# First attention of a fused kernel: maxima taken earlier, their turn moved to another PSUM bank, and the value product spread over two units

## The reference

```python
def _mha(q, k, v):                       # q: layer-normed x; k = v: the context, 1024 rows a batch
    qh, kh, vh = ...                     # 16 heads of 32 columns
    scores = einsum('bhqd,bhkd->bhqk', qh, kh) / sqrt(32)
    causal = ki <= qi + (Sk - Sq)        # Sq = 512, Sk = 1024
    scores = where(causal, scores, -10000)
    attn = softmax(scores)
    return einsum('bhqk,bhkd->bhqd', attn, vh)
x = x + _mha(_layernorm(x), ctx, ctx)
x = x + _L0_ffn(_layernorm(x))           # 8 experts, top 2
x = x + _L1_xattn(_layernorm(x), ctx)    # 8-bit rounded q, k, v and weights of attention
x = x + _L1_ffn(_layernorm(x))           # rounded, gated
```

## Time and profile before

| | us |
|---|---|
| median of 3 runs | 1800.56 |
| lowest and highest | 1793.37 and 1804.84 |
| the profiled execution | 1805.99 |
| its span, from the first to the last instruction | 1804.4 |
| mean granted TensorE clock, as a share of full speed | 0.827 |

### The profile page before, as it was taken

One profiled execution on the slowest core, in us unless ns is written; L12 is line 12 of the kernel. 1 busy time (PEld: TensorE's weight loads), 2 busy tenths in 40 slices (PEclk: granted clock), 3 DMA queues, 4 the chain that ended last, 5 costly groups with the idle time before them and its releaser, 6 DMA issues.

```text
span 1804.4 us, 23942 instructions
## 1 busy us (share of the span) xinstructions
PE 1441.1 (80%) x8264; PEld 708.2 (39%) x8312; DVE 1037.8 (58%) x1668; ACT 771.5 (43%) x1017; POOL 420.4 (23%) x318
## 2 busy tenths in 40 slices
PE   6888057777777439999999999928788888887878
PEld 3444034444444314444444444414223333334334
DVE  5777868787788511111111111156799999993895
ACT  3544357777777201111111111103677777772453
POOL 1100000000000055799994000031111111110241
PEclk9988579999999669999999999969555555557989
DMA  5556443333332099999999888843899999996001
GB/s 178 156 161 192 157 93 81 78 76 76 76 79 51 1 341 400 368 386 376 404 407 336 302 303 302 244 143 75 163 206 211 215 216 213 213 205 138 1 1 47
DMA packets 469011, 345.96 MB, mean 192 GB/s; under 512 B 382040, under 2 KB 384088, under 8 KB 468320
## 3 DMA queue, kind: packets, MB, share of 16 engines
q1 hardware_dynamic: 454160, 295.76, 59.7%
q0 software_dynamic: 10816, 40.90, 7.2%
q10 hardware_dynamic: 3984, 8.65, 1.3%
HBM read 206.32 MB, written 38.27 MB: 136 GB/s over the span
## 4 chain that ended last, share of the span: by engine, by line
PE 43%; DVE 25%; issue 13%; DMA 9%; ACT 5%; POOL 3%; SPq 1%; DVEq 1%; POOLq 0%; ACTq 0%
PE scores L891 18%; PE bank L907 9%; DVE arena L1612 6%; DVE arena L1426 6%; DMA arena<-arena 6%; DVE arena L1440 3%; DMA arena<-in_ctx 2%; PE scores L747 2%; PE bank L815 2%; ACT arena L1226 2%; PE bank L899 1%; PE bank L1078 1%; PE bank L799 1%; PE bank L936 1%; PE bank L798 1%
## 5 line engine op out<-in xcount | busy, mean ns | idle before, releaser
L1612 DVE TENSOR_SCALAR_CACHE_REDUCE arena<-scores,arena 128x1024 f32<-128x1024 f32 x256 | 318.4, 1282 | 33.5 <-ACT arena L1226 15.2
L891 PE MATMUL scores<-arena 128*128 128x512 f32 x736 | 321.7, 595 | 0.8 <-DVE arena L1549 0.8
L952 PE MATMUL scores<-arena 96*128 96x512 bf16 x512 | 263.7, 621 | 50.8 <-DVE arena L1612 38.0
L1226 ACT ACTIVATE arena<-arena 128x2048 int16<-128x2048 f32 x128 | 256.2, 2002 | 101.2 <-POOL arena L684 76.3
L1557 DVE TENSOR_TENSOR arena<-scores,arena 128x512 f32<-128x512 f32 x46 | 31.8, 692 | 447.2 <-PE scores L891 447.2
L891 PEld LDWEIGHTS scores<-arena 128*128 128x128 f32 x736 | 140.6, 191 | 178.0 <-issue 176.8
L907 PE MATMUL bank<-arena 128*128 128x512 f32 x368 | 163.3, 597 | 3.5 <-issue 3.3
L1165 ACT ACTIVATE arena<-bank 128x512 f32<-128x512 f32 (+3 forms) x256 | 118.5, 512 | 50.8 <-PE bank L799 40.4
L1426 DVE TENSOR_REDUCE arena<-scores 128x1 f32<-128x640 f32 (+3 forms) x128 | 127.6, 1019 | 14.1 <-PE scores L776 13.9
L1194 ACT ACTIVATE arena<-scores 128x512 f32<-128x512 f32 x46 | 27.5, 597 | 248.9 <-PE scores L891 248.9
L1440 DVE TENSOR_TENSOR arena<-arena 128x1024 f16<-128x1024 f32 (+2 forms) x128 | 127.7, 1018 | 1.6 <-ACT arena L1170 1.6
(11 more groups left out here) (231 smaller groups left out, 2023.6 us busy)
## 6 DMA issues: line engine op xcount, KB each, us to landing
arena<-in_L_ffn_w SPq DMA_DIRECT2D x69, 2048.0 KB, 12.4
arena<-arena SPq DMA_DIRECT2D x32, 256.0 KB, 3.2
kst_d<-arena POOLq DMA_DIRECT2D x16, 384.0 KB, 5.4
tern_d<-arena POOLq DMA_DIRECT2D x12, 512.0 KB, 7.1
arena<-kst_d SPq DMA_DIRECT2D x16, 384.0 KB, 4.3
xs_d<-arena SPq DMA_DIRECT2D x23, 256.0 KB, 3.5
arena<-xs_d SPq DMA_DIRECT2D x23, 256.0 KB, 13.4
ys_d<-arena ACTq DMA_DIRECT2D x23, 256.0 KB, 7.0
```

The lines of the kernel that those rows point to most:

```text
L891: ins = pe.matmul(scores[:, m * 1024 + half * 512:m * 1024 + half * 512 + 512], xsT[a][:, c], wa[:, m, c, half * 512:half * 512 + 512], st ...
L952: ins = pe.matmul(scores[:, s:s + 512], qhead[a][0:K3, t * P:(t + 1) * P], khead[a][0:K3, s:s + 512], start=True, stop=True)
L1226: act.activation(p16[t % PBUF], ssb[i], ACT.Exp, bias=ebias[i], scale=-1.0, accum_out=rsum[a][:, t:t + 1]).then_inc(p_ready, 1)
L1612: dve.tensor_scalar(ssb[i][:, s:s + 1024], scores[:, s:s + 1024], nsq[:, bass.ds(h, 1), t], None, ALU.mult, ALU.min, accum_out=nmx[i][:, h ...
```

## The change

- **DVE.** In step u the remainders of groups 1 to 3 now belong to unit u-1 and stand first; then come the maxima 0 and 1 of unit u+1, `finish_unit(u-1)`, maximum 2, the remainder of group 0 of unit u, maximum 3 and `split_m(u+1)`. So all four maxima of u+1 are taken ahead of three of the four subtractions of u. `take_max(u, 0)` has a new wait for `m_step`, a semaphore that DVE itself raised.
- **PE.** `turn_m(u)` opens step u; `smax(u+1, 1)` follows, then `pv` of groups 1 to 3 of unit u-1, wrapped around the first scores of unit u; `pv` of group 0 of unit u closes the step, and behind it stands `smax(u+2, 0)`.
- **Bank.** `turn_m` writes to `bank6`, `copy_m` reads it there. The wait of `smax` for `m_ready` goes; one wait for `ctxT_ready` ahead of all units is added, since `bank6` served the context before.
- **ACT.** `copy_m(u+1)` stands ahead of the last `p1` copy of unit u, behind it before.

No instruction is added to the data path and none is taken away. SP's and GpSimd's queues are as before.

```diff
@@ tensor @@
-                    if past(u, 1):
-                        pe.wait_ge(m_ready, at(u - 1))
...
-                view = scores[:, 0:512].bitcast(BF16)
+                view = bank6[:].bitcast(BF16)
...
             def att_unit(u, a, r, first, last):
                 b, rb = (a + 1) % 4, r + (a + 1) // 4
+                c, rc = (a + 2) % 4, r + (a + 2) // 4
+                d, rd = (a + 3) % 4, r + (a + 3) // 4 - 1
+                turn_m(u, a)
                 if not last:
-                    smax(u + 1, b, 0, rb); smax(u + 1, b, 1, rb)
+                    smax(u + 1, b, 1, rb)
+                if not first:
+                    pv(u - 1, d, 2, rd, not past(u, 2)); pv(u - 1, d, 3, rd, not past(u, 2))
+                st(u, a, 0, first, r); st(u, a, 1, first, r)
+                if not first:
+                    for k in range(4, KT):
+                        pv(u - 1, d, k, rd, not past(u, 2))
                 st(u, a, 2, first, r); st(u, a, 3, first, r)
                 if not last:
                     smax(u + 1, b, 2, rb)
                 st(u, a, 4, first, r); st(u, a, 5, first, r)
-                pv(u, a, 0, r, first); pv(u, a, 1, r, first)
                 if not last:
                     smax(u + 1, b, 3, rb)
                 st(u, a, 6, first, r); st(u, a, 7, first, r)
-                pv(u, a, 2, r, first); pv(u, a, 3, r, first)
-                if not last:
-                    turn_m(u + 1, b)
-                    st(u + 1, b, 0, False, rb); st(u + 1, b, 1, False, rb)
-                pv(u, a, 4, r, first); pv(u, a, 5, r, first)
-                pv(u, a, 6, r, first); pv(u, a, 7, r, first)
+                pv(u, a, 0, r, first); pv(u, a, 1, r, first)
+                if within(u + 2, UNITS):
+                    smax(u + 2, c, 0, rc)
+                if last:
+                    for k in range(2, KT):
+                        pv(u, a, k, r, first)
@@ scalar @@
+                    if g == 3 and not last:
+                        copy_m(u + 1, b)
                     act.wait_ge(exp_done, KT * u + 2 * g + 2)
...
-                if not last:
-                    copy_m(u + 1, b)
@@ vector @@
+                if t == 0 and past(u, 1):
+                    dve.wait_ge(m_step, 2 * u)
...
                 if not first:
-                    finish_unit(u - 1, not past(u, 2))
+                    for g in range(1, 4):
+                        rest_of_p(u - 1, g)
                 if not last:
                     take_max(u + 1, 0)
                     take_max(u + 1, 1)
-                rest_of_p(u, 0)
+                if not first:
+                    finish_unit(u - 1, not past(u, 2))
                 if not last:
                     take_max(u + 1, 2)
-                rest_of_p(u, 1)
+                rest_of_p(u, 0)
                 if not last:
                     take_max(u + 1, 3)
                     split_m(u + 1, False)
-                rest_of_p(u, 2)
-                rest_of_p(u, 3)
```

More of the change, by code:

```diff
@@ L842, in _ @@
                 smax(0, 0, t, 0)
-            turn_m(0, 0)
-            st(0, 0, 0, True, 0); st(0, 0, 1, True, 0)
+            smax(1, 1, 0, 0)
+            pe.wait_ge(ctxT_ready, at(NC - 1))
             sweep4(pe, UNITS, att_unit)
@@ L1155, in copy_m @@
                 act.wait_ge(m_turned, at(u))
-                act.activation(qC[b][K2:K2 + 2].rearrange("p t n -> p (t n)"), scores[:, 0:512].bitcast(BF16)[K2:K2 + 2, 0:SQ], ACT.Copy).then_inc(m_ready, 1)
+                act.activation(qC[b][K2:K2 + 2].rearrange("p t n -> p (t n)"), bank6[:].bitcast(BF16)[K2:K2 + 2, 0:SQ], ACT.Copy).then_inc(m_ready, 1)
             def att_unit(u, a, k, first, last):
@@ L1465, in att_unit @@
                     split_m(u + 1, False)
-                rest_of_p(u, 2)
-                rest_of_p(u, 3)
                 if last:
+                    for g in range(1, 4):
+                        rest_of_p(u, g)
                     finish_unit(u, False)
```

## The result

| | before | changed |
|---|---|---|
| median of 4 runs each, us | 1802.7 | 1738.68 |
| lowest and highest | 1793.37 and 1807.64 | 1736.86 and 1740.34 |
| the profiled execution | 1805.99 | 1737.13 |
| its span | 1804.4 | 1735.5 |

The ratio is 0.9671 with a 95% interval of 0.9641 to 0.97: faster by 3.3%, and inside the range forecast (1738 to 1769), but by only 0.7 us.

A forecast was written before the change was run, and what follows sets the result against it. A wait for `pv`, no full engine, was taken to bound the first attention. Steps -53.9, clock +3, first step -1, last stretch +0.5 sum to -51.4; beside the median 1800.56 that gives 1749, rounded to 1750, range 1738 to 1769.

The forecast's parts named there:

- What bounds the stage: First attention: no engine is full; a wait sets the 10.85 us unit, VectorE idling 1.68 until TensorE's `pv` is done.
- The sum of VectorE's step, 8.91: VectorE, first attention: same instructions in another order, costs taken start to start, 8.91 us a step.
- Full durations in a row: VectorE: if the new neighbours were held, 0.09 more at some six places, 0.5 a unit and 15 us in all.
- The walk: One step followed from its first remainder: `finish_unit` free by 0.26, maximum 2 without margin, the turn free by 0.1.
- The 0.14 a step: Small waits at maximum 2 and the turn, added to 8.91 for a step of 9.05 us.
- The clock in the stage: TensorE, first attention: two falls of the clock expected at 1.5 each, +3 us, with 0 and +8 as ends.
- The ends: First step -1 us (0 to -2); behind the last split +0.5, for one more `pv` tail.
- all later stages keep their length: Stages behind the first attention: no change in time expected.
- A: Scores late at maximum 2, which has no margin: 0.5 more in each step, 15 us, 1764; 17%.
- B: TensorE's clock falls in nearly every unit of the first attention, 1.6 each: 1794; 7%.
- D: Slower: TensorE stays at 1.2 GHz through the first attention, 107 us more, 1907; 4%.
- C: Another wait takes the whole place: the turn 1.7 us later than walked, 48 us, 1797; 4%.

The follow-up runs named there:

- The experiment with 0.44 us more: Changed kernel with two unread matmuls of 512 columns into bank 6 ahead of `smax(u+1, 2)`, 0.44 us a unit: 30 steps 283.15 us, median 1755.98, ratio to before 0.977.

## Why the prediction was right, step by step

- **What bounds the stage** was read rightly: the loop of split, turn, copy, scores, `pv` and finish, with 1.68 us in which VectorE had nothing to put beside it. `finish_unit` set ahead of the maxima brings 1.2 us of idle time back in each unit, and 38.8 of the 55.2 us.
- **The sum of VectorE's step, 8.91,** from start-to-start distances of the earlier trace rows: three of four steps in the loop are 8.90 to 8.94. The new neighbours start as early as the old ones did. Three remainders in a row take 2.69, which is 1.22 + 1.09 + 0.55 less twice 0.09, to a hundredth. Full durations in a row would have made the step 9.4, by the estimate in the prediction. That is what the Trainium skill's rule on emptying the pipe (VectorE: DVE Perf Modes, The DRAIN you can't avoid) gives for held operations; the trace shows the other case of that section, in which the next one starts earlier. Outside the loop and in the kernel with the loop written out the same 8.91 is in part luck. The 0.15 inside `finish_unit` isn't there, so VectorE alone would need some 0.15 less; but maximum 2 starts 0.36 behind the multiply and not 0.24 as in the loop, since its scores are not there sooner. The loop over TensorE and ScalarE, which is 8.91 too, was not in the prediction at all; it compared TensorE's work alone, 7.2, with VectorE's. In the last steps of the changed kernel, outside the loop:

```profile
493.46 0.17 DVE L1456 RECIPROCAL arena<-bank 128x4 f32<-128x4 f32 x1
493.66 0.29 DVE L1458 TENSOR_TENSOR arena<-arena 128x128 f32<-128x128 f32 x1
494.02 1.09 DVE L1434 TENSOR_REDUCE arena<-scores 128x1 f32<-128x896 f32 x1
```

- **The walk.** Maximum 2 was to start at 5.23 to 5.25 and started at 5.24. The place without margin was the right one. The 0.14 a step added for it and the turn was not needed: 30 x 0.14 = 4.2 us too many. The turn was walked wrongly: at 0.15 and free by 0.1, but it started at 0.49, since `smax(u+2, 0)` ahead of it ended late. With it `copy_m` came at 0.92 and not at 0.57, and the last `p1` copy ended at 2.05, not 1.7, so the third remainder had 0.09 to spare and not 0.4. This cost nothing in the changed kernel, where `pv` of group 1 came at 1.28, as walked (1.27).
- **The loop.** Left out of the forecast: the jump back costs VectorE 0.47 every fourth step, and the loop 2.9 us in all. In the old order, where the wait for `pv` follows the jump, every fourth step is longer by only 0.03 (10.68 and 10.65). Together with the 4.2 us too many, 271.5 was forecast for 30 steps and 270.2 measured, by two errors that cancel for the most part.
- **The clock in the stage.** Two falls at 1.5 were expected, none came in the 30 steps: 3 us less than forecast, at the lower end of that term.
- **The ends.** -1 was forecast for the first step and -2.1 measured; +0.5 for the last stretch and +1.7 measured. The clock is in both. The first step took 8.86 us at a mean clock of 0.78 in one profile of the changed kernel and 7.87 at 1.00 in the other; before it was 10.97 at 0.66 and 10.64 at 0.71. The last stretch, from the split of unit 31 to the last `finish_unit`, took 10.74 or 10.75 in all four profiles of the old order. With the new order it took 11.48 or 11.49 in all six profiles in which the clock stayed at 1.00 there, so the change costs 0.7 in it, near the 0.5 forecast. The other 0.9 is a fall of the clock behind the last split, at 514 to 518 us, which shows in the last wait for `pv`: 1.55 here, 0.62 where the clock stayed up. `finish_unit` of the last unit but one waits 1.23 for `pv`, in either case. From the changed kernel's timeline, and then one us of it, beside the same us of the kernel with `smax` 0 not ahead:

```profile
506.60 2.69 DVE L1448 TENSOR_TENSOR arena<-arena 128x1024 f16<-128x1024 f32 x3
510.52 0.56 DVE L1454 TENSOR_REDUCE arena<-bank 128x128 f32<-128x384 f32 x1 [1.23 <-PE bank L813]
...
518.72 0.56 DVE L1454 TENSOR_REDUCE arena<-bank 128x128 f32<-128x384 f32 x1 [1.55 <-PE bank L813]
```

```profile
515.00:516.00 1.00, 1.00 (x16) 1.00 (x14) 0.44 (x1) 0.97 (x3) 0.00 (x0) 0.50 0.00 0
```

```profile
515.00:516.00 1.00, 1.00 (x27) 1.00 (x25) 0.32 (x2) 1.00 (x3) 0.00 (x0) 1.00 0.00 0
```

- **The rest of the miss.** On the profiled execution -51.4 was forecast. The stage and its ends gave -55.7, the later stages +1.0, and the context stage -14.2. The last was no term of the prediction: "all later stages keep their length" was said, and held within 1 us, but of the stage ahead I took for granted that it stands still. Its clock moves it by 14 us in the kernel before, and by 9 in the one profile with the new order that has a lower clock there. Against the medians the time came out 11 us below 1750. 4 of it are the stage with its ends, as the profiles show. The other 7 are not shown stage by stage: the forecast stands beside a median of three runs of before, 1800.56, of a kernel whose runs reach from 1789.5 to 1810.9 with the mean clock, and four runs of the changed kernel lay close together, three of them at a mean clock of 0.834 or more. By the profiles at equal clock the change is worth 55 us, not 64.
- **The rivals.** A (scores late): its place was right, and it cost nothing. The experiment with 0.44 us more shows that the first matmul too many would have brought it. B and D did not come: the clock in the stage rose from 0.97 to 1.00. C did not either, though the turn was 0.3 us later than walked.

## What to carry to other kernels

When one engine waits in each unit for a chain over the others, do not shorten the chain first: ask which of the waiting engine's work doesn't need the chain, and set it between the start of the chain and its use, even if a product has to be put off by a unit for it. Then walk one step with start-to-start distances and write down each margin. The place with the smallest one is where to look for the next gain; where paths are level, all of them have to become shorter. Here 0.44 us a step taken from VectorE alone brought nothing, and with the scores earlier too it brought 5.6 us in all. Follow the chain of waits round one whole step as well: it showed a loop without VectorE that the walk had left out. Check the other margins in the first trace as well: one that was thought to be 0.4 was 0.09. Before a difference of two profiles is explained, compare the stages that the change doesn't touch, and take a second profile if they differ.

## What the runs showed of the hardware

- The granted clock of TensorE in a stage that runs the same instructions was 0.91 in one execution and 1.00 in another (475 against 515 matmuls in 140 us), and everything behind it came 14 us later.
- Filling the waits of TensorE with six matmuls of 512 columns a unit that compute nothing of use took the falls of the clock from five to none and the stage from 325.4 to 318.9 us. The Trainium skill (TensorE: Matmul & The Clock Gate, HAM oscillation) blames gaps in TensorE's work; the trace agrees, since the falls went when the gap was filled. Another section of that page (A second HAM failure mode) reports a kernel that idled for short moments between groups of matmuls and swung between the clocks for it. The new order has such moments, and all ten profiles of it have 1.00 in the 30 steps. In the last units behind them it did fall in four of the ten.
- The jump back of a loop cost VectorE 0.47 us where no wait for a slower engine came right behind it (steps of 9.38 and 8.91). It cost as much in the kernel with `finish_unit` ahead of the maxima (10.70 and 10.23), which idles 1.2 us in each step, but only behind the remainders that TensorE waits for.
- A multiply of 128x128 f32 took 0.29 us on VectorE and 0.40 on GpSimd, as this row of the timeline of GpSimd shows (the kernel with `smax` 2 earlier):

```profile
391.31 0.40 POOL L611 TENSOR_TENSOR arena<-arena 128x128 f32 x1 [8.28 <-DVE arena L1463]
```
